# Routed experts of a four-layer network: weights by one register-addressed transfer a block, scatters tied to matrix products, and table, gates and shares in smaller pieces

## What is computed

```
gout = xt @ Wg.T
topv, topi = jax.lax.top_k(gout, K)                  # K = 2 of E = 8
w = jax.nn.softmax(topv, axis=-1)
comb = jnp.einsum('tke,tk->te', jax.nn.one_hot(topi, E, dtype=x.dtype), w)
g = jnp.einsum('th,efh->etf', xt, W1) + b1[:, None, :]
v = jnp.einsum('th,efh->etf', xt, W2) + b2[:, None, :]
h = jax.nn.silu(g) * v
eo = jnp.einsum('etf,ehf->eth', h, W3) + b3[:, None, :]
out = jnp.einsum('eth,te->th', eo, comb)
```

## Time and profile before

| | |
|---|---|
| three runs | 2821.8, 2826.2, 2830.1 us |
| median | 2826.23 us |
| the profiled execution | 2810.1 us |
| its span, first to last instruction | 2808.3 us |
| TensorE busy | 2618.4 us, 93% |
| VectorE busy | 2015.0 us, 72% |
| ScalarE busy | 1675.8 us, 60% |
| GpSimd busy | 1243.6 us, 44% |
| mean granted clock of TensorE | 0.982 |

### The profile page before, as it was taken

How to read it: one execution, slowest core, us unless ns; L and a number is a source line. 1 busy time by engine, 2 the same in 40 slices (tenths; PEclk the granted TensorE clock), 3 DMA queues, 4 the chain that set the end, 5 groups by cost and what they waited for, 6 DMA issues and landing times.

```text
span 2808.3 us, 68018 instructions
## 1 busy us (share of the span) xinstructions
PE 2618.4 (93%) x24870; PEld 1791.3 (64%) x24870; DVE 2015.0 (72%) x5614; ACT 1675.8 (60%) x4127; POOL 1243.6 (44%) x1688
## 2 busy tenths in 40 slices
PE   5999999998789999999998999999989988999898
PEld 2666666665477566666665555577757765666666
DVE  6988888875444566666666899555677886887675
ACT  3888888885233667767765677543335544434565
POOL 6888888863544566211112455122343321014441
PEclk9999999999899999999999999999999999999999
DMA  3022222222256121112113544000054432435750
GB/s 112 17 54 75 75 75 75 53 54 64 85 172 187 41 47 40 24 32 47 32 32 92 170 145 140 12 1 16 1 161 143 128 107 62 89 80 145 208 168 28
DMA packets 218857, 230.81 MB, mean 82 GB/s; under 512 B 19104, under 2 KB 188768, under 8 KB 216480
## 3 DMA queue, kind: packets, MB, share of 16 engines
q1 hardware_dynamic: 207536, 193.30, 24.8%
q0 software_dynamic: 7536, 20.59, 2.6%
q10 hardware_dynamic: 3456, 12.58, 1.4%
HBM read 165.87 MB, written 75.60 MB: 86 GB/s over the span
## 4 chain that ended last, share of the span: by engine, by line
PE 70%; DVE 12%; ACT 7%; issue 4%; SPq 2%; POOL 2%; DMA 2%; another core or an unknown queue 1%; ACTq 0%; DVEq 0%; POOLq 0%
PE pb L163 61%; ACT big L961 4%; PE pb L657 3%; ACT big L160 3%; DVE big L2999 2%; DVE big L831 2%; SPq L2670 2%; PE pb L590 1%; DVE big L236 1%; PE pb L2970 1%; DVE big L3504 1%; PE pb L249 1%; DVE big L741 1%; DMA big<-parts 1%
## 5 line engine op out<-in xcount | busy, mean ns | idle before, releaser
L163 PE MATMUL pb<-big 128*128 128x128 f32 (+12 forms) x19624 | 2355.3, 327 | 122.9 <-ACT big L160 37.4
L163 PEld LDWEIGHTS pb<-big 64*128 64x128 bf16 (+4 forms) x19624 | 1481.3, 144 | 784.1 <-issue 435.1
L160 ACT ACTIVATE big<-pb 128x512 f32<-128x512 f32 (+7 forms) x1481 | 846.1, 620 | 554.8 <-PE pb L163 295.1
L160 ACT ACTIVATE big<-pb,big 128x512 f32<-128x512 f32 (+2 forms) x502 | 276.1, 585 | 435.7 <-PE pb L163 336.2
L2999 DVE TENSOR_REDUCE big<-pb 128x4 f32<-128x1024 f32 (+1 forms) x256 | 277.6, 1086 | 70.4 <-PE pb L163 65.9
L961 ACT ACTIVATE big<-big 128x256 f32<-128x256 f32 x512 | 253.7, 499 | 64.4 <-DVE big L836 63.2
L961 ACT ACTIVATE big<-pb,big 128x128 f32<-128x128 f32 (+1 forms) x512 | 256.8, 527 | 58.5 <-DVE big L816 58.3
L831 DVE CUSTOM_DVE_ANT_0 big<-pb,big 128x256 f32<-128x256 f32 x512 | 186.7, 422 | 98.2 <-PE pb L163 81.8
L174 POOL TENSOR_TENSOR big<-big 128x128 f32<-128x128 f32 x168 | 74.8, 459 | 338.3 <-DVE big L171 337.9
L187 POOL TENSOR_SCALAR big<-big 128x4 f32<-128x4 f32 (+2 forms) x99 | 26.2, 264 | 442.7 <-DVE big L182 442.5
L1040 POOL TENSOR_TENSOR big<-big 128x512 f32<-128x512 f32 x128 | 159.8, 1276 | 127.6 <-DMA big<-recip 127.4
(11 more groups left out here) (213 smaller groups left out, 2586.3 us busy)
## 6 DMA issues: line engine op xcount, KB each, us to landing
parts<-big SPq DMA_DIRECT2D x384, 96.0 KB, 2.5
big<-parts SPq DMA_DIRECT2D x72, 512.0 KB, 4.1
big<-recip SPq DMA_DIRECT2D x128, 256.0 KB, 5.4
big<-comb SPq DMA_DIRECT2D x32, 512.0 KB, 8.3
hs<-in_zero SPq DMA_DIRECT2D x10, 1472.0 KB, 8.7
parts<-big SPq DMA_DIRECT2D x192, 64.0 KB, 2.1
big<-parts ACTq DMA_DIRECT2D x24, 512.0 KB, 4.6
big<-gates SPq DMA_DIRECT2D x7, 1024.0 KB, 9.1
```

What stands on the lines that cost most here:

```text
L160: return e.activation(o, i, f, bias=bias, scale=scale)
L163: return e.matmul(o, l, r_, start=start, stop=stop, skip_group_check=True)
```

## The change

It has five pieces, all in `routed_experts` and what it shares.

1. **Weights.** The two arrays of a block's weights are one, `wx0`, with rows of 900 numbers (3600 B), and a block has one buffer of four, `WB`. SyncE loads them: `sync_weights` reads the row number into a register and issues one plain transfer of 128 rows. It waits until y of four blocks before is freed. GpSimd's 62 indirect transfers are gone. `value_load` is called without bounds.
2. **Scatters.** Each waits for a product of the unit in which it stands: three in units 2 to 8 (g0, g1, the down product), four in 9 to 15 (g0, v0, v1, down). `tail.gpsimd` stands ahead of them, `stats` behind them.
3. **Pieces.** `route` is split in `max` (four tiles at a time, where their logits are ready) and the rest, and moved; `rank` stands one unit behind `route`, after the first two products; `table` is three pieces in units 11 to 13. The exp and the shares are made once for all 24 tiles, at the end (`exp`, `share`). Chunks 1, 2 and 4 are normed on VectorE instead of ScalarE (`on_scalar`).
4. **Blocks.** Down of block j stands one step behind its up and not two; the part has one step less.
5. **Gates.** Their store stands at j = 11, their load at j = 13.

The diff, cut to its core:

```diff
         PLACE = [alloc(16).bitcast(U32) for _ in range(3)]
         HOME = [alloc(16).bitcast(U32) for _ in range(3)]
-        SHARE = [alloc(16) for _ in range(3)]
+        SHARE = alloc(48).rearrange("p (k m) -> p k m", k=2)
...
-                      14: [(0, "seed")], 15: [(2, "logits"), (2, "back"), (4, "turn")]}
-            beside = {0: [("A", "route"), (5, "stats")], 1: [(3, "logits"), (5, "normed"), ("A", "rank"), ("A", "place")],
-                      2: [(4, "logits"), (4, "back"), (5, "turn"), (3, "gate"), (6, "stats")],
-                      3: [(5, "logits"), (5, "back"), (6, "normed"), (3, "spread")],
-                      4: [("B", "route"), (6, "turn"), (3, "seed"), (7, "stats")],
-                      5: [(6, "logits"), (6, "back"), (7, "normed"), ("B", "rank"), ("B", "place")],
-                      6: [(7, "turn")], 7: [(7, "logits"), (7, "back"), ("C", "route")],
-                      8: [("C", "rank"), ("C", "place")], 9: [("C", "table")],
-                      18: [("A", "home")], 19: [("B", "home")], 20: [("C", "home")]}
-            spread_over = {1: 3, 2: 5, 3: 4, 4: 4, 5: 3, 6: 5, 7: 5, 8: 3, 9: 6, 10: 5, 11: 5}
+                      14: [(0, "seed"), (1, "max")], 15: [(2, "logits"), (2, "back"), (4, "turn")]}
+            beside = {0: [(2, "max"), ("A", "route"), (5, "stats")],
+                      1: [("A", "rank"), (3, "logits"), ("A", "place"), (5, "normed")],
+                      2: [(4, "logits"), (4, "back"), (5, "turn"), (3, "gate")],
+                      3: [(5, "logits"), (5, "back"), (3, "spread"), (6, "stats"), (4, "max")],
+                      4: [(5, "max"), (3, "seed"), ("B", "route"), (6, "normed")],
+                      5: [("B", "rank"), (6, "turn"), ("B", "place"), (7, "stats")],
+                      6: [(6, "logits"), (6, "back"), (7, "normed"), (6, "max")],
+                      7: [(7, "turn")], 8: [(7, "logits"), (7, "back"), (7, "max")], 9: [("C", "route")],
+                      10: [("C", "rank"), ("C", "place")], 11: [("C", "table_a")], 12: [("C", "table_b")], 13: [("C", "table_c")],
+                      18: [("A", "home")], 19: [("B", "home")], 20: [("C", "home")], T - 1: [("C", "exp")], T: [("C", "share")]}
+            on_scalar = (5, 6, 7)
+            three, four = (("g", 0), ("g", 1), ("y", None)), (("g", 0), ("v", 0), ("v", 1), ("y", None))
+            spread_over = {t: three if t < 9 else four for t in range(2, 16)}
...
             def tensor(e):
                 e.wait_ge(ld_wf, 16)
-                for t in range(T + 2):
+                for t in range(T + 1):
...
                     if 2 <= t < TD + 2:
                         tensor_down(e, t - 2)
-                    elif t >= TD + 2:
-                        tensor_block_down(e, t - 2 - TD)
+                    if t >= TD + 1:
+                        tensor_block_down(e, t - 1 - TD)
...
-            def gpsimd_up_in(e, j):
-                at = bass.IndirectOffsetOnAxis(ap=WROW_AT[:, j:j + 1], axis=0)
-                e.indirect_dma_start(out=WU[j % 4], out_offset=None, in_=dr["wu0"], in_offset=at).then_inc(up_in[j % 4], 16)
...
             def gpsimd(e):
                 m = 0
-                for t in range(T + 2):
+                for t in range(T + 1):
+                    if t < tail.steps:
+                        tail.gpsimd(e, t)
+                    for key, f in spread_over.get(t, ()):
+                        if m < 48:
+                            s = slots["y", t - 2] if key == "y" else slots[key, t, f]
+                            e.wait_ge(s.full, s.n)
+                            gpsimd_scatter(e, m)
+                            m += 1
                     for q, p in beside.get(t, []):
                         if p == "stats":
                             gpsimd_rstd(e, q)
-                    for _ in range(spread_over.get(t, 0)):
-                        gpsimd_scatter(e, m)
-                        m += 1
-                    if t == 12:
-                        e.wait_ge(table_made, 1)
-                        for j in range(4):
-                            gpsimd_up_in(e, j)
-                        for j in range(4):
-                            gpsimd_down_in(e, j)
...
+            def sync_weights(e, j):
+                if j >= 4:
+                    y = slots["y", TD + j - 4]
+                    e.wait_ge(y.free, y.n)
+                row = e.value_load(WROW_AT[0:1, j:j + 1])
+                e.dma_start(WB[j % 4], dr["wx0"][bass.ds(row, 128), :]).then_inc(weights_in[j % 4], 16)
...
                 e.wait_ge(table_made, 1)
+                for j in range(4):
+                    sync_weights(e, j)
                 e.wait_ge(scattered, 16 * 48)
                 for j in range(3):
-                    sync_load(e, j)
+                    sync_rows(e, j)
                 e.dma_start(WA[:, 0:4096], dr["wa1"]).then_inc(ld_wa, 16)
-                for j in range(NBLK + 3):
+                for j in range(NBLK + 1):
                     if j + 3 < NBLK:
-                        sync_load(e, j + 3)
-                    if j >= 3:
-                        sync_store(e, j - 3)
+                        sync_rows(e, j + 3)
+                    if 1 <= j and j + 3 < NBLK:
+                        sync_weights(e, j + 3)
+                    if j >= 1:
+                        sync_store(e, j - 1)
                     if j == 11:
-                        modulation.sync(e)
+                        modulation.sync_out(e)
+                    if j == 13:
+                        modulation.sync_back(e)
```

129 lines of the change are left out of this document (64 added, 65 removed).

## The result

| | kernel before | changed kernel |
|---|---|---|
| median of the runs | 2828.16 us (4, 2821.8 to 2831.0) | 2783.43 us (4, 2780.0 to 2787.1) |
| ratio, 95% interval | | 0.9845 (0.9826 to 0.9864) |
| the profiled execution, its span | 2810.1, 2808.3 us | 2784.5, 2782.7 us |
| mean granted clock | 0.982 | 0.984 |

The change saves 44.7 us where the prediction has 16.6 and a range that ends at 2788. The two profiled executions are only 25.6 us apart: that of the kernel before was 18 us under the middle of its own runs, of which it is not one. That the 18 us are more of the same is inferred. No trace shows an execution of the kernel before that took over 2811 us.

The account below looks back on a forecast made before the run. TensorE's idle and slow clock in layer 0's experts, 54 us, bound the gain; terms sum to -16.6 us, so 2793.5 on the profiled run's scale and 2809.6 from the median, forecast's own range 2798 to 2820, overall 2788 to 2833.

Parts of the forecast that it names:

- The step from the profiled run to the median: Whole kernel: the saving of 16.6 us is taken from the runs' median 2826.2, not the profiled 2810.1, giving 2809.6.
- (a): Dense stretch: GpSimd's last two neighbour-stage products go ahead of three scatters, removing 4.0 of a 4.80 us gap: -4.0 us.
- (b): Dense stretch, moved route, rank and table: waits of 3.25 and 3.04 us go, 4.0 come: -2.3 us (-6.3 to 0).
- (c): Dense stretch: scatters held by products remove 70% of 10.7 us of TensorE gaps: -7.5 us (-10.7 to 0).
- (d): Dense stretch: half of the 13.5 us of clock lost behind idle comes back: -7 us (-13 to 0).
- (e): Ahead of block 0's transposes: TensorE waits 5.9 us for the late last scatter's rows, plus 1.5 clock: +7.4 (0 to +11).
- (f): Block stretch: no indirect weight transfers on GpSimd, -7.2 us (to 0); SyncE's weights without margin, +4 (0 to +31).
- (g): Blocks, gates' round trip: SyncE no longer held, but the broadcast still precedes rows and weights 17: 0 us (-4 to +4).
- pacing does nothing: Rival, dense stretch: late signals follow the rate of indirect transfers, so (c) and (d) fall away: 2824 us, chance 0.15.
- no backlog can grow: Dense stretch, argument against the pacing rival: a held scatter stops when TensorE stops, so GpSimd cannot fall behind; no size.
- the slower rival: Block stretch: blocks wait for weights; at a landing of 8 us, 3.85 us a step, 2836.6 us; chance 0.14.
- All of it works: Whole change: (e) costs only 2, gaps and clock return nearly whole, weights in time: -37 us, 2789; chance 0.20.

Follow-up runs that it names:

- b_first: Kernel before with GpSimd's neighbour-stage products ahead of the unit's scatters, nothing else: 2810.5 us against 2819.0 on chip E.
- old_pieces: Changed kernel with max, route, rank, place and table back where the kernel before had them: 2780.9 us on chip B, ratio 0.9848.
- direct: Changed kernel without the scatters' waits, its 48 scatters replaced by plain GpSimd transfers to fixed places: 2775.6 us on chip D, ratio 0.9968.
- unheld: Changed kernel without the 48 waits of scatters on products, same number of scatters per unit: 2805.0 us on chip B, ratio 0.9927.
- after_again: Changed kernel repeated without edits on chip D: 2781.5 us, ratio 0.9988 to the kernel before.
- direct_again: Changed kernel without the scatters' waits and with 48 plain GpSimd transfers to fixed places, on chip E: 2775.5 us, ratio 0.9851.
- best_again: Changed kernel with max, route, rank, place and table in their old places and scatters ending in unit 14, on chip D: 2768.1 us, ratio 0.9942.
- unheld_again: Changed kernel without the 48 waits of scatters on products, on chip D: 2781.1 us, ratio 0.9993.

## Why the prediction was wrong

**The step from the profiled run to the median failed first.** It reads "the median of the three runs shown is 2826.2, 0.6% above it; 2826.2 - 16.6 = 2809.6". That takes the 16 us between the profiled execution and the runs as a constant that no change touches. The runs show that it is none: the distance was 18 us before the change (2828.2 and 2810.1) and is 1 us, the other way, after it (2783.4 and 2784.5), and what the change takes away depends on the chip, 44.7, 32.7 and 2.9 us on A, E and D. That step is 19.1 of the 28.1 us by which the forecast of the change was off. The 16 us were most likely more late signals; no trace of such an execution exists. On the profile's own scale the forecast was 2793.5 and the changed kernel's profiled execution had 2784.5.

**The other 9 us, by terms** (traces of A):

| term | predicted | seen |
|---|---|---|
| (a) GpSimd's order | -4.0 | gap of 4.80 gone; alone -8.5 us, interval -4 to -11 (b_first) |
| (b) route, rank, table | -2.3 | 3.25 + 3.04 gone, 3.38 + 1.03 + 3.50 come: +1.6 |
| (c), (d) held scatters, clock | -14.5 | dense stretch less the gaps of (a), (b), (e), -17.2 + 4.8 - 1.6 - 7.5: -21.5 (a remainder, not a measurement) |
| (e) last scatter | +7.4 | 7.50, and 2.2 in the first step: +9.7 |
| dense stretch in all | -13.4 | -17.2 |
| (f) weights | -7.2 and +4 | blocks -8.9, less 2.2 of (e) and -3.2 of (g): -7.9 |
| (g) gates | 0 | gap of 4.03 became 2.24; with the slow clock behind it, steps of 7.04 + 4.57 became 5.39 + 2.97: -3.2 |

(a) *Right in mechanism.* But the gap of 4.80 had hidden that route A was late. "That covers route A" failed: the two products cover 1.7 us, and rank now stands half a unit earlier, so 3.38 us show.

(b) *Wrong in sign.* Route C's wait of 3.50 was forecast as 2.5, B's as 1.5 (1.03), A's as none. old_pieces shows that undoing it costs nothing.

(c), (d) *Right in mechanism, mis-sized.* From the rows that were visible 14.5 was fair; nearly all of the waiting on it went (no "remote" over 3 us is left on ScalarE or VectorE, though five of TensorE's signals at 760 to 770 us still come 1.2 to 2.2 us late), where 70% of the gaps and half of the clock were guessed. The reading that indirect transfers back to back make signals late was right as far as it went: direct speaks for the form, unheld for the series. What the prediction couldn't see in one trace is that it depends on the chip: on C and D the same series delays nothing. The rival "pacing does nothing" is right on D (2781.1 us unheld, 2781.5 held) and wrong on B (2805.0 unheld, 2780.9 for old_pieces); on A, E and F the waits alone were not taken out.

(e) *Right in mechanism*, and the best of the sums: 5.9 us forecast, 6.7 to 7.7 measured. The forecast was for a scatter held by its own product, and the prediction's "no backlog can grow" was wrong: in the trace GpSimd is behind by units 13 to 15 and issues back to back again, which still ends after the product.

(f) *The cost of +4 was not there.* Two thirds of the block steps take 2.84 to 2.98 us and no wait names weights, so the loop over four buffers kept up, and the slower rival (2836.6) fell with it. The mean step is 3.4 us, over the prediction's own mark of 3.3; what makes it so are the first step, the gates' and some long ones that the kernel before has too (4.38, 4.57 and 6.47 us, there 4.38, 6.10 and 6.50). The landing of 4.1 us, taken from transfers of other shapes, was right. The page of after_again (columns as in the earlier trace rows):

```profile
big<-in_wx SPq DMA_DIRECT2D x31, 450.0 KB, 4.2
```

In the blocks it is 3.5 to 5.2 us there, at times over the 4.3 that the prediction's count leaves (5.7 less 0.6 and 0.8), and still no wait of TensorE names weights. What failed is the 0.13 us a block put on top. The Trainium skill, page "DMA: Bandwidth & Descriptors", section "Anatomy of one DMA", fits transfers on GpSimd's path with 2.0 us plus the bytes over 436 GB/s, which for this size would be 3.1 us by estimate. These are SyncE's, and the measured 4.2 us decides. On the saving's side, one of the four gaps that the prediction calls nameless, of 2.52 us at 823.31, names ScalarE L160. On quiet chips the term is worth nothing: first to last rows take 101.8 us before (C) and 106.2 after (D), since only lateness was to be had there.

(g) *Within its bounds*, -3.2 where -4 to +4 was given. "All of it works" (2789) was nearest of the cases, but by luck in part: on A the late first rows were not hidden (+9.7 where it has +2), and the runs had more to give back.

## What to carry to other kernels

When the profiled execution lies well below the median of its kernel, ask which waits in it vary, before the difference is carried over as a constant; a second profile, from another chip, costs one run and would have shown that they do. A series of GpSimd's indirect transfers can stall engines that have nothing to do with it, on some chips only: spread them, tie them to the progress of the engine that they would delay, and fetch what a register can address from SyncE. Before the last transfer of a held series is put beside the last product of a stage, add up what follows it, and end the series a unit earlier.

## What was not expected of the hardware

- The same program takes 2782 and 2784 us on two chips and 2819 to 2828 us on four. From 200 to 600 us a trace of either kind has the same (TensorE busy 394.1 us at a granted clock of 1.00); the difference lies where indirect transfers of GpSimd run back to back (dense stretch 114.5 or 135.0 us).
- In such a series ScalarE started a silu 19 us after the record of the product that it needs, and 0.02 us after the event of its semaphore, 1 us after the last scatter was issued. VectorE waited 2.2 us for a signal of its own. SyncE's instructions, which wait for nothing there, were slowed too: the four weight issues took 4.03 us on A and 3.23 on E, beside scatters, and 2.80 us on D and, with no indirect scatter beside them, on B (unheld) and E (direct_again).
- On the late chips 215 to 413 of the scatters' 768 landing events are in the trace, on quiet ones 765 to 768.
- Plain transfers of GpSimd, as many bytes in nearly as many packets and issued at twice the rate, delayed nothing on a late chip (E), and its trace has all 768.
- The signal of the last scatter reached SyncE 2.2 us after its issue began where no weights were in flight (best_again), and 3.5 and 4.2 us where four loads of 450 KB had just been issued (after_again, unheld_again, both on D). On A and E, with the same loads issued, it was 2.5 and 2.9 us, so the loads alone don't explain it.
